# Register loads of tile and expert numbers without bounds checks, and two numbers in one load, in a graph and mixture-of-experts layer on one core

## What is computed

```python
xn = layernorm(x)                                   # x: 6250 x 256
x = x + segment_sum(xn[src] * edge_weight[:, None], dst) @ gnn_weight   # 106250 edges
x = x + linear_attention(xn)                        # 8 heads of 64, key and value normed
h = layernorm(x)
top, idx = top_k(h @ gate_w + gate_b, 2)            # 16 experts, two for each row
moe = sum(softmax(top)[k] * (relu(h @ w1[idx[k]] + b1[idx[k]]) @ w2[idx[k]] + b2[idx[k]]) for k in (0, 1))
x = x + layernorm(h + moe) * gamma + beta
```

## Time and profile before

| | us |
|---|---|
| timed, median of 3 | 1520.85 |
| lowest, highest | 1519.32, 1523.46 |
| span of the profiled execution | 2053.1 |
| TensorE busy in it | 1168.8 |
| GpSimd busy | 1005.6 |
| VectorE busy | 651.8 |
| ScalarE busy | 406.3 |

### The profile page before, as it was taken

How to read it: one execution, slowest core, us unless ns; L and a number is a source line. 1 busy time by engine, 2 the same in 40 slices (tenths; PEclk the granted TensorE clock), 3 DMA queues, 4 the chain that set the end, 5 groups by cost and what they waited for, 6 DMA issues and landing times. The chain is left out here.

```text
span 2053.1 us, 23292 instructions
## 1 busy us (share of the span) xinstructions
PE 1168.8 (57%) x6546; PEld 848.9 (41%) x6546; DVE 651.8 (32%) x2406; ACT 406.3 (20%) x1093; POOL 1005.6 (49%) x1094
## 2 busy tenths in 40 slices
PE   0278888976423767432576324773266367576681
PEld 0144444544313655221554213552154156465670
DVE  7144344333632212223112131122212222412568
ACT  4033232321101312000211001210021022222221
POOL 2746666664365244566254663446624643204634
PEclk9899999987755888655788666887577588887885
DMA  9345444432134656233574325653364274366784
GB/s 329 97 151 185 154 153 155 141 90 62 47 98 153 217 187 216 80 91 117 176 238 143 90 92 183 196 178 90 121 220 162 85 265 143 124 210 217 244 256 138
DMA packets 155049, 323.09 MB, mean 157 GB/s; under 512 B 24769, under 2 KB 97729, under 8 KB 154785
## 3 DMA queue, kind: packets, MB, share of 16 engines
q1 hardware_dynamic: 65760, 148.16, 21.9%
q0 software_dynamic: 49296, 134.68, 21.6%
q10 hardware_dynamic: 39856, 38.67, 5.6%
HBM read 257.06 MB, written 64.36 MB: 157 GB/s over the span
## 5 line engine op out<-in xcount | busy, mean ns | idle before, releaser
L855 POOL DMA_INDIRECT ring<-normed_rows,src_sb x831 | 797.9, 960 | 780.0 <-PE ps L1512 462.2
L1661 PE MATMUL ps<-room 128*128 128x256 f32 x952 | 270.5, 435 | 115.9 <-issue 79.9
L1648 PE MATMUL ps<-room 128*128 128x128 f32 x1904 | 279.8, 300 | 70.3 <-issue 58.6
L1648 PEld LDWEIGHTS ps<-room 128*128 128x128 f32 x1904 | 260.4, 214 | 80.0 <-issue 75.2
L1661 PEld LDWEIGHTS ps<-room 128*128 128x128 f32 x952 | 199.8, 221 | 155.4 <-issue 85.3
L1445 DVE TENSOR_TENSOR desk<-ps,room 128x256 f32<-128x256 f32 x121 | 51.3, 424 | 587.6 <-PE ps L1661 293.4
L1512 PE MATMUL ps<-ring,S 128*32 128x256 f32 x1680 | 145.6, 453 | 153.0 <-DVE aggT L1116 77.9
L1539 PE MATMUL ps<-room,tT 128*128 128x512 f32 x392 | 196.7, 644 | 11.4 <-issue 11.1
L967 ACT ACTIVATE room<-ps,room 128x128 f32<-128x128 f32 x476 | 136.1, 369 | 303.5 <-remote 201.2
L846 POOL DMA_INDIRECT ring<-results_by_slot,slot_i x98 | 96.5, 984 | 146.4 <-issue 80.9
L1512 PEld LDWEIGHTS ps<-ring,S 128*32 128x32 f32 x1680 | 60.8, 125 | 211.8 <-issue 188.4
(11 more groups left out here) (226 smaller groups left out, 1247.0 us busy)
## 6 DMA issues: line engine op xcount, KB each, us to landing
room<-in_w2b SPq DMA_DIRECT2D x92, 640.0 KB
room<-in_w1b SPq DMA_DIRECT2D x92, 514.0 KB
room<-rows_by_slot SPq DMA_DIRECT2D x121, 128.0 KB
results_by_slot<-desk ACTq DMA_DIRECT2D x121, 128.0 KB
rows_by_slot<-desk ACTq DMA_DIRECT2D x6, 2432.0 KB
ring<-normed_rows,src_sb POOLq DMA_INDIRECT x831
normed_rows<-X SPq DMA_DIRECT2D x7, 896.0 KB, 8.0
result<-ring SPq DMA_DIRECT2D x49, 128.0 KB
```

What stands on the lines that cost most here:

```text
L855: pool.indirect_dma_start(out=ring[:, b % 2 * BT + m, :], out_offset=None, in_=table, in_offset=bass.IndirectOffsetOnAxis(ap=src_sb[:, b * ...
L1648: mm = pe.matmul(hps[g % 2][:, f * TS:(f + 1) * TS], w1_sb[g % WB][:, k * F + f * P:k * F + (f + 1) * P], xgT[g % 2][:, k, :], start=(k == ...
L1661: mm = pe.matmul(ops, hT[g % 2][:, f, :], w2_sb[g % WB][:, f * D:(f + 1) * D], start=(f == 0), stop=(f == FC - 1))
```

## The change

`value_load` gives way to a function `listed_value` that issues the same register load without the check. It is used for all numbers except the flag that is read once at the start. `etab` and `fresh` become the two columns of one table of pairs, `visit_tab`, and SyncE loads both numbers of a visit with one register load, before it knows whether the visit is fresh; before, it loaded `fresh`, and `etab` only within the branch.

```diff
-        etab = sb("etab", [1, VISITS], I32)
+        visit_tab = sb("visit_tab", [1, VISITS, 2], I32)
+        etab, fresh = visit_tab[:, :, 0], visit_tab[:, :, 1]
         ttab = sb("ttab", [1, VISITS], I32)
-        fresh = sb("fresh", [1, VISITS], I32)
...
+        def listed_value(eng, tab, top):
+
+            _, values = nc.values_load_multi_w_load_instructions(
+                tab, engines=[eng.engine], min_val=0, max_val=top,
+                skip_runtime_bounds_check_because="VectorE lists no tile past NTILES + 1, no expert past E and no start past NP - P")
+            return values
+
         def where_taken(eng, r, j, work, done):
...
-            expert = eng.value_load(etab[0:1, g:g + 1], min_val=0, max_val=E)
+            expert, = listed_value(eng, etab[0:1, g:g + 1], E)
...
-                    expert = eng.value_load(etab[0:1, g0:g0 + 1], min_val=0, max_val=E)
+                    expert, = listed_value(eng, etab[0:1, g0:g0 + 1], E)
...
-                    t = sp.value_load(ttab[0:1, g:g + 1], min_val=0, max_val=NTILES[p] + 1)
+                    t, = listed_value(sp, ttab[0:1, g:g + 1], NTILES[p] + 1)
...
-                new = sp.value_load(fresh[0:1, g:g + 1], min_val=0, max_val=1)
+                e, new = listed_value(sp, visit_tab[0:1, g, :], E - 1)
                 with sp.If(new > 0):
-                    e = sp.value_load(etab[0:1, g:g + 1], min_val=0, max_val=E - 1)
...
-                t = act.value_load(ttab[0:1, g:g + 1], min_val=0, max_val=NTILES[p] + 1)
+                t, = listed_value(act, ttab[0:1, g:g + 1], NTILES[p] + 1)
...
-                start = dve.value_load(base_i[0:1, b:b + 1], min_val=0, max_val=NP - P)
+                start, = listed_value(dve, base_i[0:1, b:b + 1], NP - P)
```

## The result

The changed kernel takes 1507.56 us (median of 4 runs, 1500.55 to 1509.69) where the kernel before took 1522.15 on the same chip; the ratio is 0.9882 with a 95% interval of 0.9845 to 0.9918. Two later comparisons on other chips gave 0.9905 [0.9873, 0.9937] and 0.9884 [0.9862, 0.9905]. The mean of the three is 0.989, some 17 us of 1525; the medians themselves lie 14.6, 15.1 and 18.2 us apart. The forecast was 5.2 us, with a range down to 1507.

A forecast was written before the change was run, and what follows sets the result against it. GpSimd's gathers were taken to nearly pace the main loop, with TensorE-bound visits exposed behind them. Terms of 2 + 1.2 + 0.5 + 1 + 0.5 = 5.2 us took 1520.85 to 1515.6 us, range 1507 to 1523.

The forecast's parts named there:

- SyncE's term: At the heads of seven visit lists, weights and rows issued 2.9 us earlier each; bounds 0 and 20, taken as 2 us.
- The price of a check: A check behind a register load, with its gaps, costs 0.25 us on SyncE, some 0.23 on ScalarE, 0.27 on VectorE.
- The two-number load: SyncE's load of expert number and fresh flag together takes as long as one, 0.27 us; bounds 0.27 and 0.54.
- The seam: Between the two parts, in the tail: ScalarE's stretch 1.2 us shorter without checks, rows behind it 0.5 us earlier.
- VectorE: Window-start load's check in each of 70 batches, mostly covered; bounds 0 and 7.6 us, taken as 1.
- The end: Last visits and additions: VectorE's check of 0.27 us and ScalarE's of 0.23 go, together 0.5 us.
- SyncE matters more than steady visits show: Rival: SyncE, at 3.55 of 3.73 us, cannot catch up after a wait; 8 to 16 us gained, chance 0.16.
- The collision: Rival: earlier weights bunch up with GpSimd's gathers on the DMA engines; slower, 1527 to 1531 us, chance 0.11.

The follow-up runs named there:

- the second profile of before: Another profiled execution of the unedited kernel before, used as the base of comparisons: profile of 1527.3 us, timed at 1529.07 us.
- the earlier trace: The first profiled execution of the kernel before, on which the prediction rested: it spans 2053.1 us where timed runs have a median of 1520.85.
- SyncE's part alone: Against the kernel before, only SyncE's checks gone and both numbers in one load, other engines keeping their checks: ratio 0.9876 [0.9833, 0.9918].

## Why the prediction was off

**Direction, range and base were right, the size was not.** 1507.56 lies in 1507 to 1523 by a hair, and faster was the likeliest sign. But the gain is some three times the forecast's 5.2 us, and the prediction's own sign of being wrong, "if timed runs fall by over 14 us (then SyncE, or VectorE's additions, had bound the main loop)", came up with 14.6. The mismatch of 532 us was rightly put down to the one execution. The estimate from gather prices, 1202 us to the last gather and 320 behind it, came to the right sum by two errors that cancelled: in the second profile of before the last gather starts at 1255.9, 54 us later, and 271 us lie behind it, 49 fewer. The prediction had named this as possible ("the gathers wait a few tens of us for TensorE somewhere"): they wait 47.1.

**The failed step is SyncE's term**, "The bounds are 0 and 7 x 2.9 = 20; I take 2 us, near the lower end because the 8.7 us of the earlier trace rows are what could be won". SyncE's part alone measured 19 us (12 to 25), and the other parts together at most a few. Three things were wrong in it. First, the ceiling: 8.7 us was read in an execution that was a third longer than a timed one. In the second profile of before the same wait is 24.3 us, and the one for rows 41.9 rather than 13.6. I refused stretched records as costs but used short waits of the same execution as a bound. The page of that first execution had the hint, in its group of the gathers:

```profile
L855 POOL DMA_INDIRECT ring<-normed_rows,src_sb x831 | 797.9, 960 | 780.0 <-PE ps L1512 462.2
```

GpSimd waited 462.2 us for TensorE there and waits 47.1 in the second profile. A TensorE that is late by itself, which is how I read it, finds its weights on time; that it was so there is my reading, no run shows it. Second, I compared SyncE's 3.55 us with the 3.73 of a visit, and that test was passed, yet it is a test of the rate. At the place followed the weights are in use 6.4 to 7.4 us behind their issue (4.3 to 7.5 over all profiles), longer than a visit, so what stands ahead of the issue adds to a time that is too long already. Third, I let the gathers absorb what TensorE lost; the ring is two batches deep, and where TensorE's two waits fell by 19.4 us, GpSimd's waits for TensorE fell by 13.4.

**The price of a check was about right.** Two row loads in a row stood 1.10 us apart; a pair at the changed seam lasts 1.15 in all, 0.81 apart, so a check cost 0.29 rather than 0.25. It is in SyncE's issues behind part 0, which answer to the earlier trace rows:

```profile
1341.74 0.34 SPq L738 DMA_DIRECT2D room<-in_w1b  x1
...
1343.34 1.15 SPq L727 DMA_DIRECT2D room<-rows_by_slot  x2
1345.27 0.33 SPq L738 DMA_DIRECT2D room<-in_w1b  x1
...
1346.80 1.15 SPq L727 DMA_DIRECT2D room<-rows_by_slot  x2
```

**The two-number load was mis-sized**, 0.473 us where I took 0.27 and bounded it by 0.54. "one instruction brings them" was no reason for one's price. Here the Trainium skill's figure was near: "Runtime: NRT & Kernel Launch", section "Instruction fetch mechanics", counts about 200 ns for each register loaded from HBM, and from SBUF the second register cost 0.473 - 0.279 = 0.19 us. A visit with a new expert saved 0.94 at the place followed, not 1.06. This mistake made the forecast larger, not smaller.

**The seam.** Forecast 1.2 from ScalarE and 0.5 behind it. From the last result of part 0 to the first of part 1, before (second profile) and changed:

```profile
1353.74 0.42 DVE L1445 TENSOR_TENSOR desk<-ps,room 128x256 f32<-128x256 f32 x1 [1.57 <-DMA results_by_slot<-desk]
1374.20 0.42 DVE L1445 TENSOR_TENSOR desk<-ps,room 128x256 f32<-128x256 f32 x1 [20.04 <-PE ps L1661]
```

```profile
1338.94 0.42 DVE L1451 TENSOR_TENSOR desk<-ps,room 128x256 f32<-128x256 f32 x1 [1.68 <-DMA results_by_slot<-desk]
1357.48 0.42 DVE L1451 TENSOR_TENSOR desk<-ps,room 128x256 f32<-128x256 f32 x1 [18.12 <-PE ps L1667]
```

20.46 becomes 18.54, 1.9 us less in this pair of profiles; TensorE's idle time there goes from 11.71 (11.80 in the earlier trace rows) to 11.26. The size fits, the place does not, and ScalarE's 1.2 us failed as a step: up to SyncE's first weights nothing is gained (1356.18 - 1353.74 = 2.44 us behind the last result before, 1341.74 - 1338.94 = 2.80 after), and from there 18.02 us become 15.74. By the view, the last result itself waits for the store of an earlier one, before and after (1.57 and 1.68 us), a wait that the forecast's count of ScalarE's loads left out. From ScalarE's last copy to SyncE's issue it was 6.36 us in the earlier trace rows and 7.05 in the second profile of before, and 6.73, 6.41 and 6.26 in three profiles of the changed kernel, where I had forecast 4.9. With SyncE's part alone, ScalarE's checks in place, the seam is 17.97 us; with the checks gone on ScalarE and TensorE alone it is 19.73. So what is gained here points to SyncE's burst. Other profiles of the changed kernel read 18.89 and 19.98, so a single pair carries little.

**VectorE.** I took 1 us of 0 to 7.6. Without its checks the kernel is at 0.9987, which fits. Its window addition is answered here to the earlier trace rows, by idle time until "issue" (us, times), changed:

```profile
L1122 DVE TENSOR_TENSOR aggT<-aggT,ps x70: 406/421/424, 84.6 to 1263.1; 128x256 f32 x70
...
  issue: 12.3, 20
```

In the second profile of before it is 18.2 us at 23 times, and with VectorE's checks alone gone 12.2 at 20. That kernel has six microseconds less idle time and gains no time that shows; that the gathers had it to spare is the likely reason.

**The end.** Behind the last bias addition (1465.42) 40.8 us remain in changed and 41.0 before; 0.78 us of idle time read 0.50 here. Forecast 0.5 for the whole, of which 0.3 shows.

```profile
1465.42 0.42 DVE L1451 TENSOR_TENSOR desk<-ps,room 128x256 f32<-128x256 f32 x1 [2.10 <-PE ps L1667]
...
1468.80 0.88 DVE L1490 SCALAR_TENSOR_TENSOR ring<-ring,f_mv,gamma_b 128x256 f32<-128x256 f32 x2 [0.50 <-DVEq L653]
```

**The rivals.** "SyncE matters more than steady visits show", 0.16, is what happened, at 15 to 18 us by the medians of three comparisons where it gave 8 to 16. Its argument, no time to catch up after a wait, was half the truth; the other half is the time to landing. I held the 8.7 us against it, the very number that was wrong. The collision did not come: the 831 gathers take 798.0 us together in the second profile of before and 797.8 in the changed kernel's.

**What stays open.** What a head's checks cost is measured as 6 to 7 us, but how they do it is not shown: the waits for rows scatter too much, and no head was followed. Why the weights take 4.3 to 7.5 us from issue to use at one and the same visit wasn't looked into; the DMA engines are full in that time, so a kernel that moved fewer bytes there might gain without any change on SyncE. The room for the first-layer weights is free before the result that SyncE waits for (1100.31 against 1100.90), so an order in which they are asked for ahead of that wait, for the next visit, suggests itself; neither was tried.

## What to carry to other kernels

An in-order queue that waits for one buffer and then asks for another one's content adds every register load and check behind the wait to the landing time; compare that with the time until use, and not only its length with the period of the loop. Take a ceiling for a wait only from an execution that is as long as the timed runs: a profile that is a third too long hides waits as well as inventing them. And before sizing a term from sums of waits, ask what the waiting engine holds back; behind a ring of two batches a stop is passed on.

## What the runs showed of the hardware

A register load of two neighbouring numbers takes 0.473 us and of one 0.279 us, so that merging two loads saves only 0.09 us and a gap. A profiled execution of the same code was 2053.1 us once and 1527.3 us the next time, with the same 23292 instructions. And some 0.9 us of one in-order engine's time in each of 92 visits moved a kernel of 1525 us by some 17 us, 0.2 us per visit with a new expert, while 0.27 us (an estimate) in each of 70 batches on VectorE moved it by nothing that shows. Sums of waits from single profiles of one and the same kernel differed by up to 9 us (33.2 and 42.6 for rows).
